# Two 3x3 convolutions and a spline on one core: images without zero borders, the next pair's ReLU between two evacuations

## The reference

```python
def _batchnorm(y, gamma, beta):
    mean = jnp.mean(y, axis=(0, 2, 3), keepdims=True)
    var = jnp.var(y, axis=(0, 2, 3), keepdims=True)
    inv = lax.rsqrt(var + EPS)
    return (y - mean) * inv * gamma[None, :, None, None] + beta[None, :, None, None]
w1b = w1 + lax.stop_gradient(jnp.sign(w1) - w1)     # the signs of the weights
w2b = w2 + lax.stop_gradient(jnp.sign(w2) - w2)
out = jax.nn.relu(_batchnorm(_conv3x3(x, w1b), gamma1, beta1))   # padding 1 on each side
out = _batchnorm(_conv3x3(out, w2b), gamma2, beta2)
out = jax.nn.relu(out + x)
# then, for each element: a cubic spline with 32 knots (clip, floor, table lookup, einsum over 8 ranks)
# + id_gain * out + bias
```

## Time and profile before

| | us |
|---|---|
| median of 3 runs | 1164.68 (1160.93 to 1167.83) |
| profiled execution | 1162.34 |
| its span, first to last instruction | 1160.5 |
| TensorE busy with matmuls | 1093.0 |
| VectorE busy | 954.2 |
| ScalarE busy | 909.4 |
| GpSimd busy | 138.6 |

### The profile page before, as it was taken

One profiled execution on the slowest core, in us unless ns is written; L12 is line 12 of the kernel. 1 busy time (PEld: TensorE's weight loads), 2 busy tenths in 40 slices (PEclk: granted clock), 3 DMA queues, 4 the chain that ended last, 5 costly groups with the idle time before them and its releaser, 6 DMA issues.

```text
span 1160.5 us, 51486 instructions
## 1 busy us (share of the span) xinstructions
PE 1093.0 (94%) x23818; PEld 751.4 (65%) x23818; DVE 954.2 (82%) x891; ACT 909.4 (78%) x451; POOL 138.6 (12%) x219
## 2 busy tenths in 40 slices
PE   6999999699999946999999999999999999999996
PEld 4678888578888833665666656665656766665664
DVE  5855656585665777999999999999999999999987
ACT  4435443678788627999999999999999999999971
POOL 7000000058000000011010110110110101101100
PEclk9999999899999977999999999999999999999998
DMA  6766765667767766899999989989999999999652
GB/s 229 260 257 256 278 241 224 229 236 279 278 256 281 289 249 169 189 218 228 220 218 230 218 214 236 220 216 237 215 220 222 213 230 212 225 217 219 147 134 85
DMA packets 58225, 260.95 MB, mean 225 GB/s; under 512 B 16336, under 2 KB 16336, under 8 KB 50000
## 3 DMA queue, kind: packets, MB, share of 16 engines
q1 hardware_dynamic: 48880, 209.20, 55.7%
q0 software_dynamic: 8640, 48.17, 22.7%
q10 hardware_dynamic: 544, 1.10, 0.3%
HBM read 104.29 MB, written 77.07 MB: 156 GB/s over the span
## 4 chain that ended last, share of the span: by engine, by line
PE 60%; DVE 1%; issue 1%; ACTq 0%; ACT 0%; DVEq 0%
PE tab L1161 52%; PE tab L1170 8%; ACTq L949 0%; DVE lin L1120 0%; DVE poly L1116 0%; DVE zbuf L1024 0%; DVE lin L1012 0%; DVE far_sq L1085 0%; DVE poly L1091 0%; DVE middle_mask L1046 0%; ACT zbuf L933 0%; ACT cell L941 0%; DVE lin L1018 0%; DVE offset L1032 0%; DVEq L1084 0%
## 5 line engine op out<-in xcount | busy, mean ns | idle before, releaser
L1161 PE MATMUL tab<-edge_mask,diag 128*32 128x392 bf16 x10240 | 446.8, 329 | 5.9 <-issue 5.9
L1161 PEld LDWEIGHTS tab<-edge_mask,diag 128*32 128x32 f16 x10240 | 277.1, 97 | 168.9 <-issue 28.4
L981 ACT ACTIVATE edge_mask<-cell,thr 128x6272 bf16<-128x6272 bf16 x62 | 338.6, 5508 | 0.5 <-DMA cell<-cell 0.5
L414 ACT ACTIVATE yout<-acc 128x1568 f32<-128x1568 f32 x64 | 94.2, 1472 | 163.0 <-PE acc L715 140.8
L1161 PE MATMUL tab<-middle_mask,diag 128*32 128x392 bf16 x4096 | 186.9, 332 | 26.8 <-DVE middle_mask L1046 22.9
L715 PE MATMUL acc<-band_split,w 64*64 64x392 f16 x4608 | 198.6, 330 | 9.9 <-ACT band_split L372 6.5
L715 PE MATMUL acc<-split,w 64*64 64x392 f16 x4608 | 196.5, 330 | 11.2 <-DVE w L467 9.7
L715 PEld LDWEIGHTS acc<-band_split,w 64*64 64x64 f16 x4608 | 164.3, 107 | 44.0 <-issue 14.8
L715 PEld LDWEIGHTS acc<-split,w 64*64 64x64 f16 x4608 | 154.5, 107 | 52.4 <-issue 11.8
L1161 PEld LDWEIGHTS tab<-middle_mask,diag 128*32 128x32 f16 x4096 | 110.3, 98 | 91.5 <-DVE middle_mask L1046 23.0
L524 DVE BATCH_NORM_STATS2 stats<-yout 128x392 f32 (+1 forms) x240 | 118.0, 555 | 60.8 <-ACT yout L414 60.0
(11 more groups left out here) (133 smaller groups left out, 956.2 us busy)
## 6 DMA issues: line engine op xcount, KB each, us to landing
y_scratch<-yout SPq DMA_DIRECT2D x32, 1568.0 KB, 6.2
cell<-cell SPq DMA_DIRECT2D x504, 98.0 KB, 5.0
xin<-y_scratch SPq DMA_DIRECT2D x16, 1568.0 KB, 9.1
lin<-far POOLq DMA_DIRECT2D x32, 784.0 KB, 9.5
out<-lin SPq DMA_DIRECT2D x31, 784.0 KB, 5.6
xin<-in_x SPq DMA_DIRECT2D x15, 1568.0 KB, 9.3
lin<-y_scratch SPq DMA_DIRECT2D x30, 784.0 KB, 9.5
lin<-in_x POOLq DMA_DIRECT2D x28, 784.0 KB, 7.7
```

Of the source, the lines that this page charges most:

```text
L414: act.activation(yout[b][:, :].rearrange("p (r k x) -> p k r x", r=2, k=TILES)[:, 2 * part:2 * part + 2], acc[:, 4 * part:4 * part + 4, 0: ...
L981: act.activation(mask_of(c, q)[:, :, :], cell4[c % 2][:, :, :], ACT.Sign, bias=thr[:, q:q + 1]).then_inc(sign_mask_ready, 1)
L1161: mm = pe.matmul(tab[(c + t) % 2][j * GROUP:(j + 1) * GROUP, sub, 0:SUB], keep["diag"][part][:, j % 2, t, q, :], mask_of(c, q)[:, j, sub * ...
```

## The change

1. The zero borders go. The split images are 56 rows of 56 (two bands of 30x56 in convolution 2, with the seam row). A tap at the left or right edge now takes 55 columns of each row, and a tap that would read above the first or below the last row of an image takes six rows in the one tile where that happens. The tap order changes: high part of the centre tap first, low part of the centre tap last (`TAP_PARTS`). The clearing memsets and the waits on them are gone.
2. In convolution 2 the in-place ReLU of pair g+2 (`normalise`) is issued between the first and the second evacuation of pair g. It waits for that pair's load.
3. The halo rows go from ScalarE to VectorE: scale and bias, maximum with 0, two high parts, then the low parts as before.
4. In the opening of convolution 2 ScalarE makes high parts straight from the raw image, with scale and bias divided by 64 (two more small operations in `norm`, one at the start). The first pair comes in three pieces (rows 0 to 7, 8 to 14, 15 to 27), and the plain ReLU is done in place afterwards. TensorE waits for each piece, and takes tiles 2 and 3 in high parts first.

```diff
-HP, WP = H + 2, W + 2
 TAPS = 9
+CENTRE = 4
+TAP_PARTS = ((CENTRE, 0), *((tap, part) for tap in range(TAPS) if tap != CENTRE for part in range(2)), (CENTRE, 1))
...
-BAND_PIECES = ((0, 15), (15, BAND))
+BAND_PIECES = ((0, 8), (8, 15), (15, BAND))
...
-        split = [[sb(f"split{b}{part}", [P, HP * WP], F16) for part in range(2)] for b in range(2)]
-        band_split = [[sb(f"band_split{b}{part}", [P, 2 * HB * WP], F16) for part in range(2)] for b in range(2)]
+        split = [[sb(f"split{b}{part}", [P, PX], F16) for part in range(2)] for b in range(2)]
+        band_split = [[sb(f"band_split{b}{part}", [P, 2 * HB * W], F16) for part in range(2)] for b in range(2)]
...
-            for t in (*band_split[0], *band_split[1]):
-                for r in range(2):
-                    image = bands(t)[:, r]
-                    clear(image[0:C, 0:1, 1:W + 1])
-                    clear(image[C:P, HB - 1:HB, 1:W + 1])
-                    clear(image[:, :, 0:WP:WP - 1])
...
             def first_bands(b):
-                for early, (first, end) in zip((True, False), BAND_PIECES):
-                    for t in (x_bands(b, first, end), halo[b][:, :]) if early else (x_bands(b, first, end),):
-                        act.activation(t, t, ACT.Relu, bias=cst[:, BN1_B:BN1_B + 1],
+                act.wait_ge(bn_ready, 1)
+                for n, (first, end) in enumerate(BAND_PIECES):
+                    act.activation(split_bands(b, 0, first, end), x_bands(b, first, end), ACT.Relu,
+                                   bias=cst[:, BN1_B_HI:BN1_B_HI + 1],
+                                   scale=cst[:, BN1_S_HI:BN1_S_HI + 1]).then_inc(band_hi, 1)
+                    if n == 0:
+                        continue
+                    for m in ((0, 1) if n == 1 else (n,)):
+                        act.wait_ge(band_hi, m + 1)
+                        act.wait_ge(bn_plain_ready, 1)
+                        start, stop = BAND_PIECES[m]
+                        act.activation(x_bands(b, start, stop), x_bands(b, start, stop), ACT.Relu,
+                                       bias=cst[:, BN1_B:BN1_B + 1],
                                        scale=cst[:, BN1_S:BN1_S + 1]).then_inc(normed, 1)
-                    act.wait_ge(normed, 2 if early else 3)
-                    if early:
-                        for band in range(BANDS):
-                            act.activation(halo_row(band_split[b][0], band), halo_of(halo[b], band),
-                                           ACT.Identity, scale=1.0 / SPLIT).then_inc(halo_hi, 1)
-                    act.activation(split_bands(b, 0, first, end), x_bands(b, first, end), ACT.Identity,
-                                   scale=1.0 / SPLIT).then_inc(band_early_hi if early else hi_done, 1)
+            def normalise(b, i):
+                act.wait_ge(loaded[b], 16 * (half_rounds - 1 + b) + 48 * (i - half_rounds + 1))
+                act.activation(xin[b][:, :], xin[b][:, :], ACT.Relu, bias=cst[:, BN1_B:BN1_B + 1],
+                               scale=cst[:, BN1_S:BN1_S + 1]).then_inc(normed, 1)
...
+                if conv == 1 and isinstance(g, int) and g < PAIRS + 2:
+                    act.wait_ge(loaded[b], 16 * (half_rounds - 1 + b) + 48)
+                    if split_up(g, conv):
+                        act.wait_ge(tile_done, TILES * (g - 1))
+                        first_bands(b)
+                        return
+                    normalise(b, i)
...
+                    act.wait_ge(normed, len(BAND_PIECES) + g - PAIRS)
...
-            def evacuate(g, b, i, conv):
+            def evacuate(g, b, i, conv, normalise_next):
...
+                    if part == 0 and normalise_next:
+                        normalise(b, i + 1)
...
+                    evacuate(2 * i, 0, i, conv, conv == 1 and not is_last(n))
...
+                    evacuate(2 * i + 1, 1, i, conv, conv == 1 and not is_last(n))
...
+                    so_far = g - PAIRS
+                    if isinstance(g, int) and g < PAIRS + 2:
+                        dve.wait_ge(loaded[b], 16 * (half_rounds - 1 + b) + 48)
+                    else:
+                        dve.wait_ge(normed, len(BAND_PIECES) + so_far)
+                    if split_up(g, conv):
+                        dve.wait_ge(bn_plain_ready, 1)
+                    dve.tensor_scalar(halo[b][:, :], halo[b][:, :], cst[:, BN1_S:BN1_S + 1], cst[:, BN1_B:BN1_B + 1],
+                                      ALU.mult, ALU.add).then_inc(halo_chain, 1)
+                    dve.wait_ge(halo_chain, 2 * so_far + 1)
+                    dve.tensor_scalar(halo[b][:, :], halo[b][:, :], 0.0, None, ALU.max).then_inc(halo_chain, 1)
+                    dve.wait_ge(halo_chain, 2 * so_far + 2)
+                    if not (isinstance(g, int) and g < PAIRS + 2):
+                        dve.wait_ge(tile_done, TILES * (g - 1))
                     for band in range(BANDS):
-                        dve.wait_ge(halo_hi, 2 * (g - PAIRS) + band + 1)
+                        dve.tensor_scalar(halo_row(band_split[b][0], band), halo_of(halo[b], band), 1.0 / SPLIT, None,
+                                          ALU.mult).then_inc(halo_hi, 1)
+                    for band in range(BANDS):
...
+                        for n, (first, end) in enumerate(BAND_PIECES):
+                            dve.wait_ge(band_hi, n + 1)
+                            dve.wait_ge(normed, n + 1)
...
-                    dve.wait_ge(hi_done, late(g))
+                    dve.wait_ge(hi_done, late(g) - 1)
...
+                if conv == 0:
+                    scale_hi, bias_hi = cst[:, BN1_S_HI:BN1_S_HI + 1], cst[:, BN1_B_HI:BN1_B_HI + 1]
+                    link(dve.scalar_tensor_tensor(out=scale_hi, in0=r, scalar=t, in1=par_hi[:, 0:1],
+                                                  op0=ALU.mult, op1=ALU.mult), tail)
+                    dve.scalar_tensor_tensor(out=bias_hi, in0=minus_mean, scalar=scale_hi, in1=par_hi[:, 1:2],
+                                             op0=ALU.mult, op1=ALU.add).then_inc(bn_ready, 1)
...
+                                         op0=ALU.mult,
+                                         op1=ALU.add).then_inc(bn_plain_ready if conv == 0 else bn_ready, 1)
...
+                for tap, part in TAP_PARTS:
+                    if part not in parts:
+                        continue
+                    dy, dx = tap // 3 - 1, tap % 3 - 1
+                    cols = slice(max(0, -dx), W - max(0, dx))
+                    from_cols = slice(max(0, dx), W - max(0, -dx))
+                    for r in range(2):
+                        own = slice(r * C, (r + 1) * C)
+                        for h in range(2):
+                            if conv == 0:
+                                image, first, band = rows(split[b][part], 0, H), h * BAND + k * ROWS, h
+                            else:
+                                image, first, band = bands(band_split[b][part])[:, h], 1 + k * ROWS, r
+                            top = int(dy < 0 and band == 0 and k == 0)
+                            end = ROWS - int(dy > 0 and band == 1 and k == TILES - 1)
+                            to = acc[h * C:(h + 1) * C, 2 * k + r, 0:TILE].rearrange("p (y x) -> p y x", y=ROWS)
+                            mm = pe.matmul(to[:, top:end, cols], weights[part][own, tap * C:(tap + 1) * C],
+                                           image[own, first + dy + top:first + dy + end, from_cols],
+                                           start=(tap, part) == TAP_PARTS[0], stop=(tap, part) == TAP_PARTS[-1])
...
+                    begin(k)
+                    if conv == 1:
+                        pe.wait_ge(band_hi, k + 1)
...
                 for k in range(EARLY_TILES):
+                    if conv == 1:
+                        pe.wait_ge(band_lo, 2 * k + 2)
                     taps(b, weights, conv, k, (1,)).then_inc(tile_done, 1)
+                if conv == 0:
+                    pe.wait_ge(lo_done, lo_late(g, conv))
+                    for k in range(EARLY_TILES, TILES):
+                        begin(k)
+                        taps(b, weights, conv, k, range(2)).then_inc(tile_done, 1)
+                    return
+                for k in range(EARLY_TILES, TILES):
+                    begin(k)
+                    pe.wait_ge(band_hi, len(BAND_PIECES))
+                    taps(b, weights, conv, k, (0,))
                 pe.wait_ge(lo_done, lo_late(g, conv))
                 for k in range(EARLY_TILES, TILES):
-                    wait_past(pe, evacuated, 2 * (g - 1) + 2)
-                    pe.sem_inc(tile_begun, 1)
-                    taps(b, weights, conv, k, range(2)).then_inc(tile_done, 1)
+                    taps(b, weights, conv, k, (1,)).then_inc(tile_done, 1)
```

More of the change, by code:

```diff
@@ L176, in inner @@
         def inner(t, first, end):
-            return t[:, :].rearrange("p (h w) -> p h w", h=HP)[:, 1 + first:1 + end, 1:W + 1]
+            return rows(t, first, end)
         def rows(t, first, end):
```

(1 more changed line is left out.)

72 lines of the change are left out of this document (15 added, 57 removed).

## The result

| | before | after |
|---|---|---|
| median of 4 runs each (lowest to highest) | 1164.74 us (1160.93 to 1167.83) | 1193.01 us (1191.59 to 1200.1) |
| profiled execution | 1162.34 us | 1192.02 us |
| its span | 1160.5 us | 1190.2 us |

The ratio is 1.0257, with a 95% interval of 1.0205 to 1.0308: the changed kernel is slower. The forecast was 1192 us.

A forecast was written before the change was run, and what follows sets the result against it. The prediction took TensorE, streaming columns, to bound both convolutions before the change. It added 31.8 us (convolution 2's last matmul later) and -2.2 us (convolution 1's columns) to 1162.34: 1192 us, range 1183 to 1203.

The forecast's parts named there:

- The ring: Convolution 2: second evacuation, store, load, ReLU, next second evacuation wait in a circle, 15.05 us a turn against TensorE's 12.0.
- The end: After pair 13 of convolution 2: TensorE needs 20.6 us to the last matmul, against 25.6 before; last matmul 31.8 us later.
- E(0): End of pair 0's second evacuation in convolution 2, put at 234.1 us against 233.7 before; E alone: that of any pair.
- the case on the clock: Rival, convolution 2: pauses bring TensorE's clock to 1.2 GHz in every pair, 15.4 us a pair; 1196 us, chance 0.08.
- The opening: Start of convolution 2: TensorE starts 3.1 us earlier, pair 1 only 1.0 us earlier; costed at nothing.
- The columns: Convolution 1: six of nine taps have 385 columns instead of 392, 2.9 ns less in 768 groups, saving 2.2 us.
- I take nothing for them: Convolution 1: six-row taps, shorter in one half of the array only, save nothing, with 2.2 us as the other end.
- The rule that was weighed there: Convolution 1, six-row taps: matmuls end strictly in issue order, so the saving stays 2.2 us; without it, 4.4.
- The sum: Whole kernel: 31.8 - 2.2 = +29.6 us on the profiled execution's 1162.34, giving 1192 us.
- The ring closed: Against a rival in convolution 2: load, ReLU and evacuation fit in TensorE's pair, so no ring; 1155 us, chance 0.07.
- loads that start in an empty queue: Rival, convolution 2: such loads take 8 us, making a turn 12.4 us; 1160 us, chance 0.05.
- Ragged matmuls: Rival, convolution 1: ragged PSUM writes (55 of 56) cost 2.8 us in place of saving 2.2; 1197 us, chance 0.08.

## Why the prediction was right, step by step

*The ring.* Reckoned at 15.05 us a turn, measured at 15.04 in the turn above and 15.18 in the mean. The mean is higher because some turns are long: 15.74, 15.85 and 15.50 among eleven. In the 15.85 one the second halo piece, the last of the load, landed in 8.8 us where it took 7.8 in the turn above, and the ReLU waited 7.42 us instead of 6.61: the landing makes the difference. Why some loads take 1 us more isn't known. The two first turns took 16.4 and 16.0 us where 15.6 were put down. From the store of pair 0 (231.37) to that of pair 13 (430.74) the loop took 199.4 us against 196.8 forecast.

*The end.* From pair 13's evacuation (430.71) to the last matmul 20.6 us were reckoned and 19.5 came; the pause ahead of pair 15 was 1.02 us, where 1.5 were allowed, and its 288 matmuls took 12.21. E(0) came at 231.35, where 234.1 less the 2.2 of the columns is 231.9. So errors of -0.6, +2.6 and -1.1 nearly met: the length of a turn was foreseen, but that the total is right to 1 us is in part luck, the more so as runs of one kernel spread over 7 to 9 us.

*What the engines wait for.* Forecast were two waits of TensorE (1.1 and 2 us in the case on the clock, one of 2 us in what the profile should show); there are two of 1.3. The halo rows on VectorE take 1.8 us, 1.6 reckoned (342.26 to 344.03 above), and the low parts behind them start at E + 3.84 (344.06), where 1.97 + 1.6 had them at E + 3.6. ScalarE's wait was put at "2 us and more" and is 6.5: beside the ReLU and the second evacuation it does only 2.8 + 1.46 us of work in a turn of 15, which could have been worked out.

*The opening.* TensorE starts 5.20 us after the last statistics are aggregated at 206.85, where it was 8.05: 2.85 sooner, 3.1 reckoned. Pair 1 starts 22.5 us after them, 22.6 before, so the 1.0 us expected there is missing. The chain itself is shorter by it, since ScalarE no longer has the halo rows: from the ReLU's start to the low parts' it takes 5.9 us instead of 6.9. But the load that it waits for lands 0.8 us later (12.96 us after the statistics, 12.16 before), and ScalarE, free early, waits 2.2 us for it. As forecast, none of it reaches the end. The rows, for the earlier trace rows:

```profile
206.85 0.37 DVE L648 BATCH_NORM_AGGREGATE mean_var_of_rest<-stats 128x2 f32<-128x48 f32 x1
...
210.44 2.06 ACT L353 ACTIVATE band_split<-xin,cst 128x896 f16<-128x896 f32 x2 [1.32 <-DVE cst L675]
...
212.05 14.54 PE L740 MATMUL acc<-band_split,w 64*64 64x392 f16 x288 [3.61 <-DVE band_split L478]
...
219.81 3.00 ACT L369 ACTIVATE xin<-xin,cst 128x3136 f32<-128x3136 f32 x1 [2.22 <-DMA halo<-y_scratch]
...
229.35 2.87 PE L740 MATMUL acc<-band_split,w 64*64 64x392 f16 x66 [2.76 <-DVE band_split L499]
```

*The columns: right in size by luck, wrong in cause.* The term was -2.2 us for convolution 1, and it ended 2.67 us earlier (its last store at 208.36 instead of 211.03). But that is 16 x 0.29 = 4.6 us less a later start: TensorE's first matmul is at 10.48 us instead of 9.68, the first store at 26.70 instead of 25.54, and the three pairs behind it gain 0.36 us instead of 0.87. Why was not followed. Three parts of the working fell. The first is "each 7 columns or 2.9 ns shorter", worth 0.14 us a pair: the side columns gave nothing. The second is "I take nothing for them": the six-row taps gave the other end of their range, 0.15 a pair. The third was not in the sum at all: the layout, 0.17, nearly all of it in the centre taps.

The rule that was weighed there, from the Trainium skill, "TensorE: Matmul & The Clock Gate", section "The mechanism", would by the prediction's reading have left the six-row taps without gain. The runs say otherwise: 12.11 to 11.96 us with one cut in each half. With a cut in one half alone it stays at 12.11. Each half streams at its own pace, as the starts show (141 to 148 against 165 to 172 ns). That a pair ends with the half that has more to do fits both times; with the lower cut alone not run, it is argued.

*The sum.* The last matmul of convolution 2 is 30.6 us later (450.26 against 419.65), where 31.8 - 2.2 = 29.6 was said; the part behind it came 0.9 us shorter, and the profiled execution 29.7 us longer.

*The rivals.* The ring closed, and at the reckoned length: loads that start in an empty queue land no sooner (7.7 to 8.8 us for the last halo piece). Ragged matmuls cost 0.02 to 0.04 us a pair more than whole rows, where that rival had 0.18 more and the forecast 0.14 less. The rival's 2.8 us was wrongly put in the place of the saving of 2.2: it belongs beside it, which leaves +0.6 us, 0.04 a pair, and that is what the side columns cost at either pitch. The clock did not join in: 1.00 in the loop, and 0.50 only at the opening, as in the earlier trace rows.

## What to carry to other kernels

An operation that waits for a load may be moved ahead of another only after asking what the load itself is queued behind: if that is a store of what the other operation makes, the three close a ring, and its length, added up once round, is the new time of a turn whatever the engines could do. In a profile a ring shows as no engine full and one long wait repeated at the same size. Issue loads ahead of stores that wait, and the same order of operations is free.

## What the runs showed of the hardware

- Matmuls that read seven rows of 56 fp16 values cost more when the rows begin at an odd value: at a pitch of 58 a quarter's starts come some 172 ns apart for them and 166 for the others. Rows of 55 cost as much as rows of 56 from an even value, whichever value they begin at (166 to 167 ns). Both come out if a row costs the columns of all the aligned pairs of values that it touches: 56 for the cheap ones, 58 for 56 values from an odd one. That is an estimate from these rows: 14 columns more for seven rows are 5.8 ns at 2.4 GHz, and 5.6 were measured (172.5 against 166.9). No run varied the first value by itself, and the ragged write could as well have eaten the side taps' saving, so the reading is not shown.
- The Trainium skill, "Advanced Engine Details and Errata", section "Memory Cachelines", speaks of 16-byte lines on the reading side, with a penalty for a new line at each access. An estimate from that page, for an image that begins on a line: rows of 112 bytes that touch are 49 lines for seven, rows 116 bytes apart 51.3 in the mean over the taps. But the left, centre and right taps have 51.25, 51.5 and 51.25 of them, almost the same, while the traces have the loss in the centre taps alone. So the count of lines doesn't explain the layout's gain.
- A shorter matmul in one half of the array does shorten the work if the other half has one too, even in another tile of the same pair (0.15 us a pair for 56 columns less in six groups of each half, 0.14 by the columns).
- A load issued in an otherwise idle queue right behind a store had its last piece landed in 7.7 to 8.8 us, where the earlier trace rows have 8.0 and 7.8; after 4 us without any DMA it wasn't faster.
